# A GRU with a top-2 mixture of experts: tokens sorted by expert into tiles through DRAM rows

## The reference

```python
def cell(h, x):
    gi = x @ W_ih + b_ih
    gh = h @ W_hh + b_hh
    r = sigmoid(i_r + h_r); z = sigmoid(i_z + h_z)
    n = tanh(i_n + r * h_n)
    h_new = (1.0 - z) * n + z * h          # 256 steps, one after the other

router_logits = x / norm @ router_w        # x: all states, 4096 x 512; 8 experts
rw, selected = top_k(softmax(router_logits), 2);  rw = rw / sum(rw)
for e in range(8):
    out = out + combine[:, e, None] * (x @ Wa[e] @ Wb[e])   # 512 -> 128 -> 512
result = input + out
```

## Time and profile before

| | |
|---|---|
| median of 3 runs (lowest to highest) | 1147.41 us (1147.07 to 1148.66) |
| the profiled execution | 1146.74 us |
| its span in the profile | 1144.9 us |
| granted TensorE clock, mean | 0.994 of full speed |
| busy: PE (TensorE matmuls) | 94% of the span |
| busy: DVE (VectorE), ACT (ScalarE), POOL (GpSimd) | 79%, 53%, 14% |
| moved by DMA | 38.13 MB, mean 33 GB/s |

### The profile page before, as it was taken

One profiled execution on the slowest core, in us unless ns is written; L12 is line 12 of the kernel. 1 busy time (PEld: TensorE's weight loads), 2 busy tenths in 40 slices (PEclk: granted clock), 3 DMA queues, 4 the chain that ended last, 5 costly groups with the idle time before them and its releaser, 6 DMA issues.

```text
span 1144.9 us, 49667 instructions
## 1 busy us (share of the span) xinstructions
PE 1076.9 (94%) x20690; PEld 707.4 (62%) x20690; DVE 903.4 (79%) x3475; ACT 610.2 (53%) x2189; POOL 163.7 (14%) x415
## 2 busy tenths in 40 slices
PE   1769999999999999999999999999999999999986
PEld 1445666666666666666666666666666666666654
DVE  4578888888888888888887888888788888788885
ACT  5466555555555555555555555555555555554542
POOL 2011211111111111111111111111111111110111
PEclk9899999999999999999999999999999999999999
DMA  9700011011101011110001110101111110100000
GB/s 231 186 11 21 21 31 21 21 31 30 31 21 27 18 28 30 31 26 26 22 21 30 31 30 21 31 14 28 31 30 26 25 21 21 30 21 12 12 11 20
DMA packets 47968, 38.13 MB, mean 33 GB/s; under 512 B 33296, under 2 KB 37504, under 8 KB 47744
## 3 DMA queue, kind: packets, MB, share of 16 engines
q1 hardware_dynamic: 47168, 31.81, 12.4%
q10 hardware_dynamic: 576, 3.15, 0.9%
HBM read 18.95 MB, written 8.39 MB: 24 GB/s over the span
## 4 chain that ended last, share of the span: by engine, by line
PE 89%; DVE 4%; issue 2%; DMA 1%; ACT 1%; SPq 1%; POOL 0%; POOLq 0%; DVEq 0%
PE gates L823 17%; PE ybank L866 16%; PE pairs L797 16%; PE gates L828 14%; PE obank L884 13%; PE nbank L811 7%; PE pairs L790 3%; DMA whh<-in_L_cond_W_hh 1%; PE rbank L842 1%; DVE tr L671 1%; PE rbank L850 1%; DVE pre L674 1%; ACT nn L518 0%; DVE acc L722 0%; DVE tr L676 0%
## 5 line engine op out<-in xcount | busy, mean ns | idle before, releaser
L823 PE MATMUL gates<-whh,st 128*32 128x384 f16 x4096 | 213.4, 328 | 30.6 <-DVE st L696 19.2
L510 ACT ACTIVATE rr<-pre 128x64 f32<-128x64 f32 x256 | 65.7, 257 | 294.1 <-DVE pre L674 294.0
L866 PEld LDWEIGHTS ybank<-hparts,wa 128*128 128x128 f16 x3000 | 168.4, 98 | 83.3 <-DVE y L710 62.4
L797 PE MATMUL pairs<-wx,xs 128*32 128x256 f16 x6144 | 215.1, 275 | 0.5 <-issue 0.5
L866 PE MATMUL ybank<-hparts,wa 128*128 128x128 f16 x3000 | 210.9, 220 | 3.4 <-DVE y L710 2.4
L828 PE MATMUL gates<-whh,hparts 128*32 128x384 f16 x4096 | 213.5, 326 | 0.0
L671 DVE STREAM_TRANSPOSE tr<-gates 128x256 f32<-128x256 f32 x256 | 115.1, 450 | 118.4 <-PE gates L828 118.1
L884 PE MATMUL obank<-wb,y 128*128 128x512 f16 x741 | 200.2, 379 | 0.3 <-DVE acc L722 0.3
L797 PEld LDWEIGHTS pairs<-wx,xs 128*32 128x32 f16 x6144 | 140.8, 96 | 77.2 <-issue 74.1
L823 PEld LDWEIGHTS gates<-whh,st 128*32 128x32 f16 x4096 | 96.0, 95 | 94.6 <-issue 63.1
L828 PEld LDWEIGHTS gates<-whh,hparts 128*32 128x32 f16 x4096 | 120.0, 97 | 46.4
(11 more groups left out here) (117 smaller groups left out, 1218.1 us busy)
## 6 DMA issues: line engine op xcount, KB each, us to landing
xin<-in_x SPq DMA_DIRECT2D x32, 256.0 KB
out<-outb SPq DMA_DIRECT2D x32, 256.0 KB
wih<-in_L_cond_W_ih ACTq DMA_DIRECT2D x4, 768.0 KB, 9.2
whh<-in_L_cond_W_hh SPq DMA_DIRECT2D x16, 192.0 KB, 12.8
wih<-in_L_ffn_Wb SPq DMA_DIRECT2D x1, 2048.0 KB, 14.1
wih<-in_L_ffn_Wa SPq DMA_DIRECT2D x8, 128.0 KB, 8.2
whh<-in_L_ffn_Wa SPq DMA_DIRECT2D x8, 128.0 KB, 5.2
xs<-xh SPq DMA_TRANSPOSE x58, 2.5
```

What stands on the lines that cost most here:

```text
L797: mm = nc.tensor.matmul(bank[32 * j:32 * j + 32, P:3 * P], turned(b, k, ph)[:, t0:t0 + 2 * B], wx[:, pw, k, j, :], start=False, stop=(k == ...
L823: nc.tensor.matmul(g[32 * j:32 * j + 32, 0:3 * P], st[:, k, :], whh[:, 1, k, j, :], start=False, stop=False, skip_group_check=True)
L866: mm = nc.tensor.matmul(y_at(m)[:, 0:P], wa[:, pw, k, e, :], hparts[:, f % HB, k, :, ph * B:(ph + 1) * B], start=(n == 0), stop=(n == 3 * ...
```

## The change

The first 31 blocks no longer go through all eight experts. They are taken in seven chunks of 7, 6, 4, 4, 4, 4 and 2 blocks. For each chunk the tokens are sorted by expert, twice each, into tiles of 128 rows that belong to one expert alone: a chunk of nb blocks gets 2 nb + 7 tiles, whatever the routing. That is 21, 19, 15, 15, 15, 15 and 11 tiles, 111 in all. The last block goes through all eight experts as before (8 items).

- Routing of block f: ScalarE's `gather_states` at phases 0 and 1; then a DMA transpose by SP (`turn_states`, phase 2) puts the states, token by row, into one of eight buffers `hft`. `logits` on TensorE, `rank_experts` on VectorE and `choose` on POOL are at phase 2. `count_ranks` on TensorE (phase 3) counts, by matmuls with a triangle and with ones, how many earlier tokens of the chunk chose each expert, and ScalarE reads it (`read_rank`). The sum of squares is now made from `hft`: `add_parts` on POOL (128x512, phase 4), `sum_squares` on VectorE (phase 5), `invert_norm` (5), `weigh` and `scale_weights` (6).
- Planning: at phase 4 of a chunk's last block POOL runs `plan(c)`, 24 small instructions that each wait for the one before, to find each token's row and each tile's expert; then `scatter(c)`, two indirect DMAs a block, which write the token rows of `hft` into DRAM (`state_rows`). By the program's own planner, worked out on paper, the plans stand at steps 60, 108, 140, 172, 204, 236 and 252.
- A tile t: POOL gathers the expert's weights (all parts of Wa and Wb, 4 KB a row, 524 KB) from a DRAM table with an indirect DMA (`load_weights`); SP loads the rows with a DMA transpose (`load_tile`, 262 KB), four steps ahead, into rings of three. TensorE, ScalarE and VectorE do `expert_down`, `split_y` and `expert_up` as before. ScalarE's `read_rows` copies the result to SBUF, and SP stores it (`store_tile`, 262 KB) as rows in DRAM. There is one tile every second step. By the planner they stand at 70 to 110, 118 to 154, 156 to 184, 186 to 214, 216 to 244, 246 to 265 and 266 to 276 (from step 256 on one item a step); the last block's eight experts stand at 277 to 284, and the loop ends at 299.
- Back to tokens: for each block POOL gathers its two result rows a token (`gather`, two indirect DMAs of 262 KB), SP loads the input again (`load_left`), and three steps later VectorE's `sum_rows` adds the two, times their weights, in two instructions; SP stores.
- Once: SP writes the weight table (8 DMAs, step 20) and clears the DRAM rows (40 DMAs, steps 22 to 61).

```diff
+CHUNKS = (7, 6, 4, 4, 4, 4, 2)
-    DOWN, UP, ADD = S + 4, S + 5, S + 5
+    N_TILES = [2 * nb + NE - 1 for nb in CHUNKS]
+    def at(f, s):
+        return (f + 1) * S + s if f < NB - 1 else T + 2 * s
+    STEP_US, ITEM_US = 3.7, 1.3
+    PLAN_AT = [at(FIRST_BLOCK[c + 1] - 1, 4) for c in range(len(CHUNKS))]
...
+    for c, nb in enumerate(CHUNKS):
+        step = max(step, after(PLAN_AT[c], 8 + 2.4 * nb + 8))
+        step += step % 2 if step < T else 0
+        for _ in range(N_TILES[c]):
+            item_step.append(step)
+            step += 2 if step < T else 1
+        read = max(read, after(item_step[-1] + 2, 4))
+        for f in range(FIRST_BLOCK[c], FIRST_BLOCK[c + 1]):
+            gather_step[f] = read
+            read = after(read, 5)
...
+            def turn_states(f):
+                sp.wait_ge(hf_ready, 2 * (f + 1))
...
+                sp.dma_start_transpose(hft[f % HFT].rearrange("t (g p) -> t g p", g=2 * K),
+                                       hf[:, :, :, :].rearrange("p w k t -> p (w k t)")).then_inc(hft_turned[f % 2], 16)
+            def load_tile(t):
...
+                wait(sp, y_done, t - RING + 1)
+                sp.dma_start_transpose(tile_x[t % RING].rearrange("p (g t) -> p g t", g=2 * K),
+                                       state_rows[c % 2][row:row + P, :]).then_inc(tile_x_loaded[t % RING], 16)
+            def store_tile(t):
...
+                sp.wait_ge(rbuf_ready, t + 1)
+                sp.dma_start(out_rows[c][row:row + P, :], rbuf[t % 2]).then_inc(rbuf_stored[t % 2], 16)
...
+            def add_parts(f):
+                pool.wait_ge(hft_turned[f % 2], 16 * (f // 2 + 1))
+                wait(pool, ssum_ready, f)
+                nc.gpsimd.tensor_tensor(hsum[:, :], hft[f % HFT][:, 0:D], hft[f % HFT][:, D:2 * D], ALU.add
+                                        ).then_inc(hsum_ready, 1)
+            def scatter(c):
...
+                for f in range(FIRST_BLOCK[c], FIRST_BLOCK[c + 1]):
+                    pool.wait_ge(hft_turned[f % 2], 16 * (f // 2 + 1))
+                    for t in range(2):
+                        nc.gpsimd.indirect_dma_start(
+                            state_rows[c % 2][:, :], bass.IndirectOffsetOnAxis(slots[:, f, t:t + 1], 0), hft[f % HFT], None
+                        ).then_inc(scattered[c % 2], 16)
+            def load_weights(t):
...
+                wait(pool, o_done, t - RING + 1)
+                nc.gpsimd.indirect_dma_start(
+                    tile_w[t % RING], None, w_table[:, :], bass.IndirectOffsetOnAxis(w_rows[:, t:t + 1], 0)
+                ).then_inc(tile_w_loaded[t % RING], 16)
...
+            for n in range(STEPS):
+                if n % S == X_AT + 1 and n // S + FIRST < NB:
+                    split_x(n // S + FIRST)
+                if n in route_at[2]:
+                    choose(route_at[2][n])
+                if item_at.get(n + 4, ITEMS) < TILES:
+                    load_weights(item_at[n + 4])
+                if n in plan_at:
+                    plan(plan_at[n])
+                    scatter(plan_at[n])
+                if n in gather_at:
+                    gather(gather_at[n])
+                if n in route_at[4]:
+                    add_parts(route_at[4][n])
+                if n in route_at[5]:
+                    invert_norm(route_at[5][n])
...
+            def read_rows(t):
+                act.wait_ge(o_done, t + 1)
+                wait(act, rbuf_stored[t % 2], 16 * (t // 2))
...
+                nc.scalar.activation(rbuf[t % 2], o_at(t)[:, :], ACT.Copy).then_inc(rbuf_ready, 1)
...
+            def sum_squares(f):
+                dve.wait_ge(hsum_ready, f + 1)
...
+                nc.vector.tensor_tensor_reduce(squares[:, :], hsum[:, :], hsum[:, :], 1.0, 0.0, ALU.mult, ALU.add,
+                                               ssum[:, :]).then_inc(ssum_ready, 1)
+            def sum_rows(f):
+                i = f % 2
+                dve.wait_ge(got_loaded[i], 32 * (f // 2 + 1))
...
+                nc.vector.scalar_tensor_tensor(out=acc[:, :], in0=got[2 * i], scalar=wts[:, f, 0:1], in1=left[i][:, :],
+                                               op0=ALU.mult, op1=ALU.add).then_inc(sum_step, 1)
...
             def beside(n):
...
+                if n in route_at[2]:
+                    rank_experts(route_at[2][n])
+                if n in item_at:
+                    split_y(item_at[n])
+                if n in route_at[5]:
+                    sum_squares(route_at[5][n])
+                if n - SUM in gather_at:
+                    sum_rows(gather_at[n - SUM])
...
             def expert_down(m):
                 wait(pe, ylo_ready, m if m <= LAST else m - 1)
+                if m < TILES:
+                    pe.wait_ge(tile_w_loaded[m % RING], 16 * (m // RING + 1))
+                    pe.wait_ge(tile_x_loaded[m % RING], 16 * (m // RING + 1))
```

More of the change, by code:

```diff
@@ L267, in gru_moe_kernel @@
         N_RW_SPLITS = len(SPLITS)
-        wb_split_at, wa_split_at = {}, {}
         for half in range(2):
[L270 to L277, removed]
+            split_wa(half)
+        for e in range(NE):
+            split_wb(e)
         def splits_before(n):
@@ L282, in gru_moe_kernel, with chunk_of_tile, wait_scattered @@
         X_AT = 6
+        SUM = 3
+        def chunk_of_tile(t):
+            return max(c for c in range(len(CHUNKS)) if FIRST_TILE[c] <= t)
+        def wait_scattered(eng, c):
+            rows = sum(2 * CHUNKS[i] for i in range(c % 2, c + 1, 2))
+            eng.wait_ge(scattered[c % 2], 16 * rows)
         def past(n):
@@ L610, in _ @@
                 beside(n)
-            last_experts()
+            for n in range(T, STEPS):
+                beside(n)
         @block.vector
@@ L725, in add_expert @@
+            def add_expert(e):
+                own = xin[:, (NB - 1) % XIN, :]
+                dve.wait_ge(o_done, TILES + e + 1)
+                if e == 0:
+                    dve.wait_ge(comb_step, 3)
+                wait(dve, acc_done, e)
+                nc.vector.scalar_tensor_tensor(out=own if e == NE - 1 else last_acc[:, :], in0=o_at(TILES + e)[:, :],
+                                               scalar=comb[:, e:e + 1], in1=own if e == 0 else last_acc[:, :],
                                                op0=ALU.mult, op1=ALU.add).then_inc(acc_done, 1)
@@ L738, in beside @@
                     split_weights(N_GRU_SPLITS + n - 1 - LATE)
-            def last_experts():
-                for m in range(LAST, T):
-                    split_y(m)
-                    add_expert(m - 1)
-                    if m == LAST + 3:
-                        rank_experts(NB - 1)
-                add_expert(T - 1)
             split_first(0)
```

537 lines of the change are left out of this document (375 added, 162 removed).

## The result

The changed kernel takes **1398.61 us** (median of 4 runs, 1384.84 to 1409.84) where the kernel before took 1147.24 (1146.85 to 1148.66) on the same chip. The longest of the four counts as a slow run; the other three have a median of 1393.08 us, and from them comes the ratio of 1.2148, interval 1.2043 to 1.2254, that later runs are held against. It is slower by a fifth.

A forecast was written before the change was run, and what follows sets the result against it. The prediction took the recurrence, 4.14 us a step, as the bound, with experts under it. Its sum was 1146.7 - 20.4 + 10 + 86 + 9 + 76 = 1307.8, so 1308 us, range 1205 to 1430.

The forecast's parts named there:

- rival A: Whole kernel: chain floor kept, POOL late seven times, DMA-paced tail; 1308 us, chance 0.70.
- The floor: Recurrence from st to st: 4.14 us a step even without experts, with the expert work lying under it.
- 20.4 us of excess: Recurrence time over 255 steps of 4.14 us, all given back by fewer expert items: -20.4 us, other end 0.
- Rival D: Recurrence: unloaded TensorE shortens the chain to 3.7 us a step, kernel faster at about 1090 us; chance 0.04.
- The waiting place: VectorE's sum_squares waits for add_parts behind plan and scatter on POOL in seven chunks' last blocks: +86 us, ends 52 and 167.
- Rival B: POOL's plan and scatter end before VectorE asks, so only the tail counts: 1213 us, chance 0.09.
- The clock: TensorE at granted clock 0.50 after each of seven stalls, one state part doubled: +9 us, ends 0 and 15.
- VectorE's new work: VectorE in the recurrence: sum_rows exceeds its free time, some steps sharing with sum_squares; +10 us, ends 0 and 15.
- The tail: After the recurrence: 21 tiles, eight experts and six blocks' sums take 102 us where 26 were; +76, ends +30 and +98.
- Transfers inside the recurrence: 6.55 MB in eight steps takes 29 of 33.1 us, loads issued four steps ahead, so 0 us.
- Rival C: Recurrence: transfers can't keep up, TensorE waits for its tile; +238 us at 150 GB/s, near 1540; chance 0.17.

The follow-up runs named there:

- experiment eight: The kernel before with only the first of three terms of its expert matmuls, everything else the same; 1128.95 us, ratio 0.9827.
- experiment three: The changed kernel with one added wait, so POOL's add_parts starts only after VectorE's last state instruction of phase 4; 1379.34 us, ratio 1.2017.
- Experiment five: The changed kernel with the tail's input loads two steps earlier; 1429.13 us, and on the third chip 1427.66 beside the changed kernel's 1441.02.
- one to three: The changed kernel with add_parts ahead of plan, 1378.97 us; or later plan and spread scatter, 1345.09; or a wait before add_parts, 1379.34.

## Why the prediction was right, and where its sum was short

The forecast was rival A, slower with a kept floor, late POOL and a long tail: 1308 us against 1384.8 profiled and 1398.6 in the median, inside the range. The larger mechanisms were the forecast's; 77 of the 91 us that it fell short by are in the profiled execution. (The terms of its sum add up to 1307.3, not 1307.8, which changes nothing.) That the time fell inside the range is in part the luck of the chip: on the third one the same program took 1441.02 us, above the 1430 where the range ends, through held steps that the sum has no term for.

**The floor** held. 4.14 us is the step in the windows with TensorE busy 2.69 us, and experiment eight shows it without any of the change: cover removed, floor unmoved. The 20.4 us of excess that the sum gave back in full were too many: with the load lightened, experiment eight still has 7.3 of them. Rival D fell, and with it the reading of 94% busy as "bound by TensorE".

**The waiting place** was right in place and, but for the last gap, in size: predicted stalls 19.0, 16.4, four of 11.2 and 6.1 us, measured excesses 19.9, 16.8, 11.2, 12.1, 11.2, 11.2 and 13.3, 95.5 for 86. `plan` took 9.1 us for 9.2; one indirect issue 0.96 us and 0.30 to the next, so 1.27 for 1.2. Of the missing 9.5 us 7.2 are the last gap, where two gathers (2.6 us) and a wait of 1.8 us stood between the plan and the add. Rival B fell. The Trainium skill's figure of about 1 us (DMA: Bandwidth & Descriptors, Latency and other measured facts) would have given 74 us; the period is a quarter longer, and the trace decides.

**The clock** cost 8.9 us for 9: every step behind a gap is 5.4 us, with a granted clock of 0.50 over the first two of them and of 0.54 to 0.72 over the others.

**VectorE's new work** was put at 10 us, and here lies the first term that was short. The whole remaining excess is 41.2 us. Of the 23.0 at phases 4 and 3, 19.3 went with one wait in experiment three and so are no matter of VectorE's load; how the other 18 divide was not tried. The prediction priced `add_parts` by its 1.17 us on POOL and asked only who waits for it. It did not ask what runs on VectorE in the meantime. The kernel before had waits that put POOL's wide additions behind VectorE's state split; the new one starts as soon as its inputs are there, across the state split. Experiment three put such a wait back and the stretch was gone. The Trainium skill (SBUF — State Buffer, Who interferes with whom) says that a VectorE instruction with two inputs in SBUF contends with a GpSimd instruction that reads SBUF, and that the later one blocks fully. By that rule the split, issued first, should not have been the one to stand still: the profile has it begin 0.54 us ahead of POOL's add and end just after it. That the two collide agrees; the order does not, though a POOL span's start is rough. (In the rows at the end of this document the instruction that starts later is the stretched one both times.)

**The tail** was the largest miss: 112 us more for 76. Its tile part was near: 84 us for 75, at 261 GB/s for the mixture instead of the 300 taken for its plain part, and 4.2 us a tile instead of 3.9. Its second part was 54 us for 27. I had priced the last six blocks by their bytes at 300 GB/s. The chain shows they are not byte-paced: SP issues a block's input load after the store of the block before, 7.2 to 7.5 us pass to its landing, and the 9.5 to 9.8 us from block to block (7.7 for the last) are a serial round trip at a share of 0.41. Experiment five took 13 to 19 us of it back by order alone.

**Transfers inside the recurrence** were put at 0. For the first profile that fits: without the weights the last `st` stands 2 us earlier. In the profiles of one to three it doesn't: `sum_rows` stands there 7 to 10 us for an input load that comes late, ahead of the recurrence, a wait that neither the sum nor a rival had. On the third chip the same program's excess is 49 us larger, 27 of them in seven steps where TensorE and VectorE were held without a wait that the profile can name. Whether the transfers hold them is not shown. Rival C named a price for transfers inside the recurrence, but as tiles that come late; in neither profile of the changed kernel does TensorE stand for a tile's transfer. The remaining 14 us between the profiled execution and the median are spread of this kernel's runs, which no profile here accounts for.

## What to carry to other kernels

Find the floor in a stretch without the work you mean to save; if the step is as long there, the saving is worth only the excess over it. When work enters a queue, price it three times: what waits behind it in the queue, what shares a memory path with it on another engine, and which waits in the old code existed only to time it. A tail of few blocks is priced by its round trips, not by its bytes.

## What the runs showed of the hardware that was not expected

- A VectorE subtraction with both inputs in SBUF (128x64, 225 ns) took 1.78 us beside a POOL add of 128x512 (1.16 us). Timed into VectorE's gap, POOL's add stretched nothing. Two of POOL's and VectorE's wide instructions stretch each other: POOL's add, begun 0.21 us into a first VectorE sum of 0.75 us, took 1.56 us for the 1.17 of the earlier trace rows, and the second sum, begun under the add, took 1.53 for the 0.76 that it takes alone. The changed kernel's timeline:

```profile
591.07 0.75 DVE L1062 SCALAR_TENSOR_TENSOR acc<-whh,wts,left 128x512 f32<-128x512 f32 x1
591.28 1.56 POOL L613 TENSOR_TENSOR xh<-x,xh 128x512 f16<-128x512 f32 x1 [2.57 <-DVE hparts L988]
591.86 1.53 DVE L1065 SCALAR_TENSOR_TENSOR left<-whh,wts,acc 128x512 f32<-128x512 f32 x1
```

- An indirect DMA of 256 KB keeps POOL for 0.96 us and 0.30 more to the next, each time: 1.27 us.
- The kernel before measures 1147 to 1149 us on every chip used. The changed one measured 1385 to 1410 on one and 1439 to 1449 on another. There state matmuls came in threes, and VectorE's transposes stood 31.8 us in six steps although the matmuls that they wait for had ended. 302 MB, most of it plain loads, at 241 GB/s did not do that to the kernel before. The cause is open.
